# Attention of a two-layer kernel: tiles of two heads in turn, both heads' values in one bank, and one projection for both

## What is computed

```python
qkv = (x @ qkv_w.T).reshape(Bb, Ss, 3, H, D)
q = _rope(q, c, s); k = _rope(k, c, s)
scores = jnp.einsum('bhqd,bhkd->bhqk', q, k) * SCALE
kb = -p * jnp.log1p(a * dist)
attn = jax.nn.softmax(scores + kb[None], axis=-1)
out = jnp.einsum('bhqk,bhkd->bhqd', attn, v)
return out.reshape(Bb, Ss, H * D) @ out_w.T
...
xn = _layernorm(x, axis=-1)
s = _L0_attn_ref(xn, ...)
g = _silu(_L0_ffn_ref(xn, ...))
x = x + s * g
```

## Time and profile before

| | us |
|---|---|
| median of 3 runs | 1789.51 (1787.14 to 1791.3) |
| the profiled execution, its own time | 1783.67 |
| its span in the trace | 1781.8 |
| first stage, to the first score of the attention | 402.6 |
| attention, to about | 1519 |
| layer 1 | the rest |

### The profile page before, as it was taken

How to read it: one execution, slowest core, us unless ns; L and a number is a source line. 1 busy time by engine, 2 the same in 40 slices (tenths; PEclk the granted TensorE clock), 3 DMA queues, 4 the chain that set the end, 5 groups by cost and what they waited for, 6 DMA issues and landing times. The chain is left out here.

```text
span 1781.8 us, 39061 instructions
## 1 busy us (share of the span) xinstructions
PE 1638.8 (92%) x12100; PEld 901.2 (51%) x12100; DVE 1494.9 (84%) x3032; ACT 1150.7 (65%) x1755; POOL 1405.2 (79%) x805
## 2 busy tenths in 40 slices
PE   3879989848999999999999999999999999799888
PEld 2435655423555555555555555555555555356556
DVE  7878979976898988989889898898989888788821
ACT  5636444537887778787787787877878776322043
POOL 5676847857999999999999999999999997554411
PEclk9899999988999999999999999999999999899999
DMA  5467856778899889889889889889889988100001
GB/s 153 137 182 195 226 156 183 196 213 170 173 194 217 186 189 218 186 178 233 184 180 232 176 188 220 189 187 217 191 181 220 197 175 178 51 1 1 1 8 41
DMA packets 732915, 294.09 MB, mean 165 GB/s; under 512 B 629089, under 2 KB 696675, under 8 KB 732849
## 3 DMA queue, kind: packets, MB, share of 16 engines
q1 hardware_dynamic: 730816, 290.33, 72.5%
q0 software_dynamic: 2048, 3.15, 0.9%
HBM read 101.34 MB, written 58.85 MB: 90 GB/s over the span
## 5 line engine op out<-in xcount | busy, mean ns | idle before, releaser
L1274 POOL TENSOR_TENSOR probs_lo<-probs 128x1024 bf16<-128x1024 f32 x512 | 954.2, 1894 | 80.1 <-ACT probs L1242 79.1
L1242 ACT ACTIVATE probs<-scores,neg_max 128x1024 f32<-128x1024 f32 x512 | 589.2, 1151 | 219.3 <-DVE neg_max L1161 210.8
L1161 DVE CUSTOM_DVE_ANT_0 scores<-score_ps,bias_tab 128x1024 f32<-128x1024 f32 x512 | 620.5, 1220 | 83.1 <-issue 77.1
L1075 PE MATMUL score_ps<-x 128*128 128x512 bf16 x1024 | 308.9, 384 | 33.0 <-PEq L284 19.6
L1091 PEld LDWEIGHTS turn_ps<-ident_bf,probs 128*128 128x128 bf16 x4096 | 261.4, 98 | 146.3 <-issue 56.5
L1091 PE MATMUL turn_ps<-ident_bf,probs 128*128 128x128 bf16 x4096 | 314.2, 220 | 0.2
L1110 PE MATMUL pv_ps<-probs_t_hi,v_hi_lo 128*128 128x512 bf16 x1024 | 263.6, 380 | 0.3 <-DVE share L1193 0.3
L1249 ACT COPY probs_t_hi<-turn_ps 128x1024 bf16<-128x1024 bf16 x256 | 254.0, 992 | 0.0
L440 POOL TENSOR_TENSOR qk_parts<-rotated,qk_parts 128x1024 bf16<-128x1024 f32 x64 | 137.5, 2153 | 81.9 <-ACT qk_parts L875 81.4
L1176 DVE COPY probs_t_hi<-turn_ps 128x1024 bf16<-128x1024 bf16 x256 | 172.8, 675 | 0.8 <-PE turn_ps L1091 0.8
L1083 PE MATMUL score_ps<-x 64*128 64x512 bf16 x1024 | 155.9, 383 | 0.0
(11 more groups left out here) (218 smaller groups left out, 2302.1 us busy)
## 6 DMA issues: line engine op xcount, KB each, us to landing
x<-qk_parts SPq DMA_DIRECT2D x192, 256.0 KB, 3.4
qk_parts<-qk_parts SPq DMA_DIRECT2D x256, 128.0 KB, 2.6
v_hi_lo<-v_parts SPq DMA_DIRECT2D x64, 256.0 KB, 3.1
bias_tab<-bias_by_distance SPq DMA_DIRECT2D x64, 240.0 KB, 3.9
v_parts<-bias_tab SPq DMA_DIRECT2D x52, 256.0 KB, 2.8
probs_t_lo<-probs_lo SPq DMA_TRANSPOSE x512, 3.2
g<-in_x SPq DMA_DIRECT2D x4, 512.0 KB, 5.8
dispatch<-dispatched SPq DMA_DIRECT2D x8, 256.0 KB, 4.0
```

What stands on the lines that cost most here:

```text
L1075: pe.matmul(sp_[n % 2][:, cs], QB[s][:, q], KK[s][:, cs], start=True, stop=False)
L1161: v.tensor_tensor_reduce(SB[n % 2][:], sp_[n % 2][:], TB[s][:, j:j + S], -SCALE, 3.0e38, ALU.add, ALU.min, neg_max[:, n % 16:n % 16 + 1]). ...
L1242: act.activation(PR[n % NP][:], SB[n % 2][:], ACT.Exp, bias=neg_max[:, m:m + 1], scale=-1.0, accum_out=row_sum[:, m:m + 1]).then_inc(exped, 1)
L1274: g.tensor_tensor(LQ[n % NL][:], PR[n % NP][:], PRB[n % NP], ALU.subtract).then_inc(low_made, 1)
```

## The change

- **Order of tiles.** Within an iteration the tiles go head 0 (4 tiles), head 1 (4), head 0 (4), head 1 (4): `head_of(n) = n // 4 % 2`, `tile_of(n) = n // 8 % 2 * 4 + n % 4`. A half now holds four tiles of either head, the same queries of both.
- **Products by the values.** Both heads' values lie in one tile `VP`. Each product by the high part now has 64 columns, head 0 in the lower and head 1 in the upper column half, and all of a half goes into one bank: 32 products where there were 16. The low part is as before.
- **Sums divided out ahead of the projection.** DVE splits the 8 inverse sums of a half into three bf16 parts (`part`, five operations on 128 x 8). PE turns them into rows (`turn_sums`, one transpose with 24 columns, at j = 3), ACT copies the rows (`take_rows`), PE spreads them (`spread_sums`, four products with 24 rows, at j = 4), ACT copies the result (`take_spread`, 128 x 512), and DVE multiplies (`normalise`, j = 6).
- **One projection for both heads.** ACT makes the high part (`take_out`), DVE the rest (`out_low`), PE's `out` has 12 products, and DVE adds one 128 x 512 tile (`add_share`). POOL has no `add_share` any more.
- **Loads.** Queries and keys at tiles 10 and 14 for tiles 16 and 20. Pieces of the bias tables at other tiles. The values in two halves behind `pv_half` and `pv_ready`, in a single buffer.
- **First stage.** The four Silu activations of the gate move to ACT's tail in the attention; clearing `SACC` moves from POOL to DVE; the last unit of queries and keys and the four loads of `freq` are issued by ACT; the output weights are stored for pairs of heads, half as large; POOL makes the selection matrix `SEL`.

```diff
             def by_v(it, hh, j):
-                for k in range(j % 2 * 4, j % 2 * 4 + 4):
-                    if j < HI_STEPS:
-                        r = BT * h + 4 * i
-                        mm = pe.matmul(ov[i][:], VV[h][:, k, :], PT[:, r:r + 4, k, :], start=(k == 0),
-                                       stop=False, skip_group_check=True)
+                each = 2 if j < HI_STEPS else 4
+                for k in range(j % HI_STEPS * each, j % HI_STEPS * each + each):
+                    for a in parts:
+                        for s in range(2):
+                            r = BT * c + 4 * s
+                            mm = pe.matmul(ov[c][s * DH:s * DH + DH], VP[:, k, s, a, :], src[:, r:r + 4, k, :],
...
+            def turn_sums(it, hh):
+                pe.wait_ge(split, at(it, 10, 5 * (hh + 1)))
+                pe.transpose(ov[1 - c][:].bitcast(BF16)[0:3 * BT, 0:P], I3[c][:].rearrange("p a n -> p (a n)"),
+                             ident16[:]).then_inc(rows_ready, 1)
+            def spread_sums(it, hh):
+                pe.wait_ge(rows_out, at(it, 2, hh + 1))
+                for i in range(4):
+                    mm = pe.matmul(by_tile[1 - c][:, i, :], K.SEL[:, i, :], RW[c][:], start=(i == 0), stop=True,
...
             def out(it, hh):
-                for c in range(2):
-                    pe.wait_ge(ot_ready[c], at(it, 2, hh + 1))
+                pe.wait_ge(ot_ready, at(it, 2, hh + 1))
...
             def step(it, u, there):      # DVE
                 if there(n) and j == OUT_STEP:
-                    take_out(it, hh)
+                    normalise(it, hh)
+                if there(n) and j < 3:
+                    if j == 0:
+                        invert(it, hh)
+                    else:
+                        part(it, hh, 2 * j - 1)
                 if there(u + LS):
                     bias_max(it, u + LS)
                 if there(n - BT) and j == 1:
                     add_share(it, hh - 1)
-                if there(n) and j == 2:
-                    invert(it, hh)
-                if there(n) and j == PROJ_STEP:
-                    scale_share(it, hh)
+                if there(n) and j < 3:
+                    part(it, hh, 2 * j)
+                if there(n) and j == OUT_STEP:
+                    out_low(it, hh)
...
-        LOADS = (BT - 2, U - 2)
-        PIECES = {BT - 3: [(0, 0)], BT - 1: [(0, 1)], BT: [(0, 2)], BT + 1: [(0, 3)],
-                  U - 3: [(1, 0)], U - 1: [(1, 1)], 0: [(1, 2)], 1: [(1, 3)]}
+        LOADS = (U - 6, U - 2)
+        PIECES = {6: [(0, 0)], 8: [(1, 0)], U - 6: [(0, 1)], U - 5: [(0, 2)], U - 3: [(0, 3)],
+                  U - 2: [(1, 1)], U - 1: [(1, 2), (1, 3)]}
```

More of the change, by code:

```diff
@@ L282, in before_heads, with write_unit @@
     GATHERED = MIX_AT[-1] < UNITS - 2
+    def write_unit(eng, n):
+        g4, w, b, c = unit(n)
+        eng.wait_ge(lo_ready, n + 1)
+        for m in range(4):
+            rows = K.qkscr[b * G + g4 * 2 + m // 2, m % 2].rearrange("k (a d) s -> d (k a) s", a=2)
+            eng.dma_start(rows[:, 4 * w:4 * w + 4, c * CH:c * CH + CH],
+                          parts[n % QR][32 * m:32 * m + 32]).then_inc(qk_wr[n % QR], DMA)
     with nc.Block() as block:
@@ L325, in _ @@
             load_halves(1)
[L327 to L331, removed]
-                    rows = K.qkscr[b * G + g4 * 2 + m // 2, m % 2].rearrange("k (a d) s -> d (k a) s", a=2)
-                    sp.dma_start(rows[:, 4 * w:4 * w + 4, c * CH:c * CH + CH],
-                                 parts[n % QR][32 * m:32 * m + 32]).then_inc(qk_wr[n % QR], DMA)
             def after_step(step):
@@ L817, in normalise @@
                 ins.then_inc(xn_ready, 1)
+            for i in range(P // (DH // 2)):
+                act.dma_start(freq[32 * i:32 * i + 32, :], io["freqs"].rearrange("(p o) -> p o", o=1)).then_inc(fr_in, DMA)
             normalise(0)
@@ L906, in _ @@
                     scale_rows(b)
-            for b in range(B):
-                n = slice(b * BT, b * BT + BT)
-                if b == 0:
-                    act.wait_ge(mixed, B)
-                    act.wait_ge(o_out, NJOB)
-                act.activation(K.G0[:, n, :], K.G0[:, n, :], ACT.Silu)
+            write_unit(act, UNITS - 1)
 def load_scores_in(sp, K, ix, s):
@@ L939, in attend @@
     qk_in, tab_in = K.qk_in, K.tab_in
-    v_in = [sem(f"av_in{s}") for s in range(2)]
+    v_in = [sem(f"av_in{i}") for i in range(2)]
     s_ready, biased, exped = sem("s_ready"), sem("biased"), sem("exped")
@@ L958, in attend @@
     OL = [sb(f"out_t_lo{i}", [P, CH], BF16) for i in range(2)]
-    SH = sb("share", [P, 4, D])
-    ot_hi = [sem(f"ot_hi{c}") for c in range(2)]
+    IB = [sb(f"inv_spread{i}", [P, CH]) for i in range(2)]
+    I3 = [sb(f"inv_parts{i}", [P, 3, BT], BF16) for i in range(2)]
+    RW = [sb(f"inv_rows{i}", [3 * BT, P], BF16) for i in range(2)]
+    rest = sb("inv_rest", [P, BT])
     neg_max, row_sum = sb("neg_max", [P, 16]), sb("row_sum", [P, 16])
@@ L1143, in step @@
                     out(it, n // BT)
+                if there(n) and n % BT == ROWS_STEP:
+                    turn_sums(it, n // BT)
+                if there(n) and n % BT == SPREAD_STEP:
+                    spread_sums(it, n // BT)
                 if there(n) and n % BT < V_STEPS:
@@ L1274, in low @@
                 g.tensor_tensor(LQ[n % NL][:], PR[n % NP][:], PRB[n % NP], ALU.subtract).then_inc(low_made, 1)
-            def add_share(it, h):
-                g.wait_ge(scaled, at(it, 4, 2 * h + 3))
-                g.sem_inc(add_begun, 1)
-                row = (it % B) * BT
-                acc = K.SACC[:, row:row + 4, :] if isinstance(row, int) else K.SACC[:, bass.ds(row, 4), :]
-                g.tensor_tensor(acc, acc, SH[:], ALU.add).then_inc(added, 1)
             def step(it, u, there):
@@ L1286, in step @@
                     low(it, u + LT)
-                if there(u) and u % BT == BT - 1:
-                    add_share(it, u // BT)
-            g.nop().then_inc(added, 1)
             run(g, step)
```

281 lines of the change are left out of this document (163 added, 118 removed).

## The result

| | before | after |
|---|---|---|
| median, us | 1790.4 (1787.14 to 1794.26, 4 runs) | 2016.97 (2012.8 to 2021.17, 4 runs) |
| ratio of the two | | 1.1274, 95% interval 1.1255 to 1.1293 |
| profiled execution, us | 1783.67 | 2016.84, its span 2015.1 |

What follows compares the result with a forecast made beforehand. PE was taken to set the pace, held up by DVE once per half. Attention +87 us, bias tables +12 and first stage and ends -6 gave +93 on 1789.5: 1883 us, range 1822 to 1930.

Steps and rivals of the forecast that it cites:

- divided products: Values' products, steps j = 0 to 3: each change between whole-array and divided products costs 0.10 to 0.11 us; +0.66 us per half.
- turned and spread sums: PE's one transpose with 24 columns and four products with 24 rows: +0.50 us per half, bounds 0.28 and 0.9.
- the projection's inputs: At j = 6 `out_low` queues behind `bias_max` on DVE, so PE's projection waits for its input: +0.33 us per half.
- the five parts on DVE: Five 128 x 8 operations, 0.1 to 0.2 us each, ready before PE asks: costed at nothing; late ones 0.1 to 0.3.
- bias tables: Last table piece for head 0 lands 1 to 3 us late, 7 times: +12 us in all (0 to 20).
- first stage and ends: `freq` arriving sooner for DVE's first work, -4 us, plus changes at the end: -6 us in all (0 to -8).
- steps by the values of 0.99 us: Sign of a right forecast: a step of values' products on PE takes 0.99 us; 0.88 would mean rival 2.
- halves of 18.5: Sign of a right forecast: one half of the attention (eight tiles) takes 18.5 us, from about 17.1.
- None of the three was the pacer: Claim that POOL, DVE and ACT do not set the pace; their changed work matters only where PE waits for DVE.
- Rival 1: The projection's inputs come in time, so PE's waits there go: -0.4 us per half, 1770 us; chance 0.09.
- rival 2: Divided products are free, so 0.66 and 0.22 of the sums go: 1827 us; chance 0.10.
- rival 3: Loads set the pace: queries and keys come 1 us late twice per iteration, about 1930 us; chance 0.12.

## Why the prediction was wrong, step by step

| term, per half | predicted | measured | by |
|---|---|---|---|
| divided products | +0.66 | +0.64 | alone, in the kernel before |
| turned and spread sums on PE | +0.50 | +0.48 | left out |
| the projection's inputs | +0.33 | +0.13 | rows below |
| the five parts on DVE | nothing | +2.06 | moved to POOL |
| half in all | +1.4 | +3.30 | PE's timeline |
| bias tables, in all | +12 us | +26 us (+34 with the parts on POOL) | left out; PE's timeline |
| first stage and ends, in all | -6 us | about 0 | see below |

The sum of the measured ones: 62 x 3.30 = 205, and 26 for the tables, gives 1790 + 231 = 2021, measured 2017. With the parts on POOL it is 62 x 1.24 + 34 = 111, measured 109. Of that 1.24 the three terms 0.64, 0.48 and 0.13 make up all. (The upper end of the prediction's own sum is 1789.5 + 124 + 20 = 1933, not 1920; it makes no difference to the outcome.) Of the signs that it named, steps by the values of 0.99 us came (1014.19 to 1015.18); halves of 18.5 came only with the parts on POOL, and POOL was busy 71.8%, not 81 to 83.

**The step that failed** is the sentence that DVE's parts are "ready a step earlier than PE asks" and are costed "at nothing", at 0.1 to 0.2 us each by the row of the reciprocal. Its own figures left no step: the last part would begin at 1.9 us and PE ask at 2.1. In the run PE waits 23.7 / 34 = 0.70 us of each half for the last part, and 52.4 / 34 = 1.54 us for scores that `bias_max` frees late. The duration was taken from an operation of the same shape and in the same memory, and that was the wrong likeness, since the reciprocal does not wait for POOL. What decides is the kind of operation, where its operands lie, and what POOL does meanwhile. POOL was 93% busy, nearly all of it with low parts, so most such operations had to meet one; in the changed kernel three of the five do on average. In the attention of before, DVE has no cast or difference with all its matrices in SBUF. Its first stage has: one addition of 128x1024 takes 1.22 us alone, and beside a POOL instruction, in the same trace,

```profile
358.85 3.04 DVE L648 TENSOR_TENSOR g<-g,s 128x1024 f32<-128x1024 f32 x1
```

```profile
358.65 2.14 POOL L440 TENSOR_TENSOR qk_parts<-rotated,qk_parts 128x1024 bf16<-128x1024 f32 x1
```

It ends 1.10 us behind POOL's, about as much time as it needs alone, as if it had stood still until POOL was through. So the rows to see the wait were there, in another stage. With them the bound is one low part, 1.9 us, for each of the five. The true size lay between: the five take 3.6 us per half on DVE, 2.8 over their 0.8 alone, and 2.06 of the 3.6 reach PE. "None of the three was the pacer" was the second mistake: DVE at 84 to 90%, with `bias_max` in order behind the parts, passes delays on to PE. Even of the 1.0 us of five reciprocals, 0.41 arrived.

**The divided products and the sums** came out within 0.02 us each. The first was worked from the earlier trace rows; the second was chosen between bounds of 0.28 and 0.9, so that it came so close is partly luck.

**The projection's inputs** have the right mechanism and the wrong size. The wait is there, 1.2 to 1.3 us of idle PE for `out_t_lo`, and all of the halved projection went into it:

```profile
1007.70 0.60 PE L1096 MATMUL score_ps<-x 64*128 64x512 bf16 x4
1008.24 0.62 PE L1104 MATMUL turn_ps<-ident_bf,probs 128*128 128x128 bf16 x8
1010.03 0.23 PE L1160 MATMUL pv_ps<-wo_parts,out_t_hi 128*128 x1 [1.17 <-DVE out_t_lo L1243]
...
1011.59 0.59 PE L1088 MATMUL score_ps<-x 128*128 128x512 bf16 x2
```

The projection starts at H + 2.33 (H being 1007.70), not H + 2.77, and the second pair at H + 3.89. The term that was most off is the start of `bias_max`, taken as 0.74 behind the scores, from a place where DVE stood idle and waited for them; here it is 0.44. The prediction named that value and its result, +0.03, and chose the other. PE also starts 0.05 behind its operand, not 0.20. And the halves of the kernel before are not "all alike". Every second one has no such wait, as its neighbour of the earlier trace rows shows:

```profile
1042.15 0.61 PE L1083 MATMUL score_ps<-x 64*128 64x512 bf16 x4
1042.69 0.62 PE L1091 MATMUL turn_ps<-ident_bf,probs 128*128 128x128 bf16 x8
1043.15 0.22 PE L1127 MATMUL pv_ps<-wo_parts,out_t_hi 128*128 x1
...
1045.86 0.60 PE L1075 MATMUL score_ps<-x 128*128 128x512 bf16 x2
```

There the second pair starts at H + 3.71, in the other kind at H + 4.00, on average at H + 3.86; in the changed kernel it is H + 3.89 and H + 4.10 by turns, H + 3.99. So the term is +0.13 in place of +0.33.

**Tables.** Right in kind (DVE waits at a new pair, seven times), under half its size: 26 / 7 = 3.7 us each, and 34 / 7 = 4.9 with the parts on POOL, above the 1 to 3 worked out.

**First stage and ends.** DVE's first work came 2.1 us sooner, at 8.85 in place of 10.99, and yet the attention's first scores came at 402.74 where they came at 402.57. The gain was absorbed behind it, and nothing was run to say where. Behind the last projection the changed kernel has 1.5 us less. **The rivals:** none happened. Rival 1 fails by the wait above, rival 2 by the divided products' price, rival 3 by PE's waits, in which queries and keys are missing in the changed kernel. They come up only as the other waits go: 2.8 us of 700 with the parts on POOL, 12.3 with `out_low` moved as well.

## What to carry to other kernels

Take the price of a new small operation from a row of the same kind of operation with its operands in the same memories, not from one of the same size, look for it in every stage of the trace, and look at what POOL does beside it: on VectorE, a cast or a difference that lies wholly in SBUF can last until POOL's running instruction ends. What helped here was to put such work on POOL behind its own instruction; DVE's operations with an operand in PSUM kept their durations. ScalarE was not tried for it, though its exponential, from SBUF to SBUF, kept 1.15 us beside the same low parts. Where a wait goes, name what is late next: here a projection halved in PE's time was given back whole at its input, a merged step at the next wait, and a moved operation at the next scores; time was gained only where nothing else was late behind it, by a copy moved to an engine with slack ahead of the place where PE stood.

## What was not expected of the hardware

- A DVE cast or difference of 128x8, with all operands in SBUF, took 0.15 to 0.17 us alone and up to 1.9 beside POOL's low part of 1.89, ending 0.02 to 0.03 us after it. A reciprocal of the same size kept 0.20 us beside it, also in the kernel with five more of them per half.
- A change between whole-array and divided products costs about 0.1 us on PE each time: 0.64 us for six of them in the kernel before, 0.19 for two.
- Twice in a row PE idled about 1.9 us ahead of a projection; the first time the granted clock stayed at 1.00, the second it was 0.50 over the 2.6 us that followed. In the changed kernel it stayed at 1.00 from 700 to 1400 us, with idle times up to 2.3 us. By the Trainium skill, TensorE: Matmul & The Clock Gate, Part 1, the gate follows how busy PE has been; by that rule, the rows agree that idle time can be followed by the lower clock, and they show that it need not.
